# Self-attention's row maxima, turned into rows by one matmul, copied by ScalarE, and added by one-hot weights in the 32-row strips

## The reference

```
q, k, v = heads(x @ Wq), heads(x @ Wk), heads(x @ Wv)     # bias and rotary turn in the first only
scores  = einsum('bhqd,bhkd->bhqk', q, k) / sqrt(16)
probs   = softmax(scores)                                  # exp(scores - max over k), then divided by the sum
x       = x + concat(einsum('bhqk,bhkd->bhqd', probs, v)) @ Wout
```

## Time and profile before

| | us |
|---|---|
| three executions, median (lowest, highest) | 1425.71 (1423.34, 1426.29) |
| the profiled execution, its own time | 1422.83 |
| span of the profile | 1420.9 |
| TensorE clock granted, mean of the span | 0.983 of full |
| PE busy, share of the span | 94% |
| DVE, ACT, POOL busy | 70%, 55%, 26% |

### The profile page before, as it was taken

One profiled execution on the slowest core, in us unless ns is written; L12 is line 12 of the kernel. 1 busy time (PEld: TensorE's weight loads), 2 busy tenths in 40 slices (PEclk: granted clock), 3 DMA queues, 4 the chain that ended last, 5 costly groups with the idle time before them and its releaser, 6 DMA issues. The chain is left out here.

```text
span 1420.9 us, 41741 instructions
## 1 busy us (share of the span) xinstructions
PE 1329.2 (94%) x15796; PEld 1197.8 (84%) x15796; DVE 1001.7 (70%) x2423; ACT 782.4 (55%) x1569; POOL 371.4 (26%) x458
## 2 busy tenths in 40 slices
PE   5999999799979999998999999889999999689887
PEld 5889889699969999998898999768888888578777
DVE  5888888455554545453777777677777777788885
ACT  2655555355545445453555565545555556377786
POOL 1212212011111212110000000055555555134442
PEclk9999999899989999999999999999999999899999
DMA  6000000031000000001000000020000000000000
GB/s 228 3 2 0 0 0 3 7 113 36 30 31 1 1 0 0 0 1 32 22 3 0 0 0 1 2 84 17 16 15 15 15 8 2 1 16 22 30 23 30
DMA packets 16477, 28.72 MB, mean 20 GB/s; under 512 B 3616, under 2 KB 7712, under 8 KB 16000
## 3 DMA queue, kind: packets, MB, share of 16 engines
q1 hardware_dynamic: 16384, 27.44, 5.9%
HBM read 23.24 MB, written 4.19 MB: 19 GB/s over the span
## 5 line engine op out<-in xcount | busy, mean ns | idle before, releaser
L830 DVE TENSOR_REDUCE a_row_max<-a_S 128x4 bf16<-128x512 f32 (+1 forms) x384 | 246.8, 683 | 54.4 <-PE a_S L993 28.8
L723 ACT ACTIVATE a_probs<-a_S 128x512 f32<-128x512 f32 x384 | 208.9, 595 | 112.8 <-PE a_S L1006 60.3
L172 POOL TENSOR_TENSOR all_var_eps<-all_moments,all_ln_eps 128x2 f32<-128x2 f32 x96 | 25.1, 262 | 714.7 <-DVE all_moments L167 714.7
L961 PE MATMUL a_S<-a_qm_hi,all_odd_split 32*128 32x256 f32 x1536 | 187.8, 302 | 7.3 <-DVE a_row_max L830 4.2
L961 PEld LDWEIGHTS a_S<-a_qm_hi,all_odd_split 32*128 32x128 f32 x1536 | 131.5, 183 | 41.5 <-issue 26.2
L687 POOL TENSOR_TENSOR a_shifts<-a_add_mask,a_row_max 128x512 bf16<-128x512 bf16 x128 | 131.0, 1040 | 118.1 <-DVE a_row_max L830 118.1
L952 PE MATMUL a_S<-all_odd_split,a_qm_hi 32*128 32x128 f32 x1536 | 126.8, 283 | 1.7 <-DVE all_odd_weights L938 1.7
L180 DVE TENSOR_SCALAR all_xn<-all_x_res,all_moments,all_rstd 128x256 f32 (+1 forms) x192 | 99.8, 561 | 19.6 <-POOL all_rstd L174 18.8
L961 PE MATMUL a_S<-a_qm_lo,all_odd_split 32*128 32x256 f32 x768 | 108.7, 277 | 0.0
L1019 PE MATMUL a_AV<-a_probs,a_v_pad 128*32 128x128 f32 x3072 | 103.8, 276 | 0.0
L952 PEld LDWEIGHTS a_S<-all_odd_split,a_qm_hi 32*128 32x128 f32 x1536 | 99.8, 185 | 2.6 <-DVE all_odd_weights L938 2.5
(11 more groups left out here) (250 smaller groups left out, 3865.9 us busy)
## 6 DMA issues: line engine op xcount, KB each, us to landing
all_cx<-in_ctx SPq DMA_DIRECT2D x32, 256.0 KB, 2.8
all_x_res<-in_x SPq DMA_DIRECT2D x8, 512.0 KB, 7.7
out_x<-all_x_res SPq DMA_DIRECT2D x16, 256.0 KB, 2.0
b_routed_wi<-in_L_ffn_wi_W SPq DMA_DIRECT2D x1, 1024.0 KB, 5.2
b_routed_wo<-in_L_ffn_wo_W SPq DMA_DIRECT2D x1, 1024.0 KB, 8.0
all_even_weights<-in_L_ffn_W_fc SPq DMA_DIRECT2D x1, 1024.0 KB, 4.9
all_even_weights<-in_L_ffn_W_proj SPq DMA_DIRECT2D x1, 1024.0 KB, 6.9
a_a_raw<-in_L_attn_Wqkv SPq DMA_DIRECT2D x1, 512.0 KB, 4.3
```

The lines of the kernel that those rows point to most:

```text
L723: act.activation(probs[:, t % STEPS, :], S2[t % 2][:], ACT.Exp, scale=DH ** -0.5).then_inc(exp_ok, 1)
L830: dve.tensor_reduce(row_max[:, t % 4, :], S1[t % 2][:].rearrange("p (h k) -> p h k", h=QH), AXX, ALU.max).then_inc(max_ok, 1)
L961: pe.matmul(S2[t % 2][:, c * HV * P:(c + 1) * HV * P], k[par][strip, c, tok], q[par][strip, c, b].rearrange("p h t -> p (h t)"), start=(c ...
```

## The change

Only the self-attention stages change (`not cross` in the code).

- `row_max` becomes a 128 x 128 bf16 tile, zeroed once by POOL; `max_step` writes the four maxima of step t to its columns 32(t mod 4) to 32(t mod 4)+3.
- `turn_max`, new on PE, once a pair of steps: one product with `row_max` as weights and the negated identity moving. It puts the negated maxima into rows (row 32j+h is head h of the step in strip j) in the first 128 columns of bank S1_0. It waits for both maxima of the pair. It stands before `transposes` at t = 0, between `queries` and `av_step` at t = 2, in the middle of `keys` at t = 4, between `values` and `av_step` at t = 6. In the last group it stands right before `av_step` at t = 2 and 6, for lack of the projections.
- `take_max`, new on ACT, once a pair: copies those 128 columns to `maxT` (two buffers, bf16). It stands behind the second exp and behind the copy of `out_high`, if there is one.
- In `scores`, behind the passes of S2, eight products of 32 rows take the place of the eight of `shift_step`: the weights are one column of the constant `strip_rows` (one-hot, 32 rows) broadcast to 128 columns, the moving operand is the strip of `maxT`. They alternate between the two strips and S2 banks of the pair. Both `s2_full` marks now come at their end.
- `scores` waits for `take_max` of the pair before, for S1_0 and for `maxT`, and no longer for anything between S2 and the shift.
- One more constant is loaded at the start (a DMA on SP) and converted by DVE.

```diff
     def __init__(self, nm, a):
-        self.from_dram = {k: a[k] for k in ("ident", "head_mask", "turn_sign")}
+        self.from_dram = {k: a[k] for k in ("ident", "head_mask", "turn_sign", "strip_rows")}
...
         dve.tensor_copy(tiles["ident_b"][:], tiles["ident"][:])
+        dve.tensor_copy(tiles["strip_rows_b"][:], tiles["strip_rows"][:])
...
-    row_max = sb("row_max", [P, 4, QH], FP32 if cross else BF16)
+    row_max = sb("row_max", [P, 4, QH] if cross else [P, P], FP32 if cross else BF16)
+    maxT = None if cross else [sb(f"maxT{i}", [P, P], BF16) for i in range(2)]
...
+            if not cross:
+                pool.memset(row_max[:], 0.0).then_inc(zeroed, 1)
...
+            def take_max(G, t):
+
+                N = G * (STEPS // 2) + t // 2
+                act.wait_ge(maxt_full, N + 1)
+                at_least(act, s2_full, G * STEPS + t - 2)
+                act.activation(maxT[t // 2 % 2][:], S1[0][:, 0:P], ACT.Copy).then_inc(maxt_ok, 1)
...
+                    if not cross and t % 2 == 1 and has_step(G, t):
+                        take_max(G, t - 1)
...
-                dve.tensor_reduce(row_max[:, t % 4, :], S1[t % 2][:].rearrange("p (h k) -> p h k", h=QH),
+                dst = row_max[:, t % 4, :] if cross else row_max[:, 32 * (t % 4):32 * (t % 4) + QH]
+                dve.tensor_reduce(dst, S1[t % 2][:].rearrange("p (h k) -> p h k", h=QH),
...
+            def turn_max(G, t):
+
+                pe.wait_ge(max_ok, G * STEPS + t + 2)
+                pe.matmul(S1[0][:, 0:P], row_max[:], neg_ident_b[:], start=True, stop=True).then_inc(maxt_full, 1)
+
             def scores(G, t, parity):
...
                     at_least(pe, max_ok, T)
+                    if not cross:
+                        at_least(pe, maxt_ok, T_2(G, t))
...
                     at_least(pe, exp_ok, T - 2)
+                    if not cross:
+                        pe.wait_ge(maxt_ok, T_2(G, t))
...
+                if second and not cross:
+                    for at in range(QH):
+                        for u in range(2):
+                            b, j, _ = place(t - 2 + u, parity)
+                            strip = slice(32 * j, 32 * j + 32)
+                            last = pe.matmul(S2[u][:, at * P:(at + 1) * P], strip_rows[strip, at:at + 1].to_broadcast([32, P]),
+                                             maxT[(t // 2 - 1) % 2][strip, :], start=False, stop=(at == QH - 1),
+                                             skip_group_check=True)
+                            if at == QH - 1:
+                                last.then_inc(s2_full, 1)
...
-                    else:
-                        last = pe.matmul(part, row_max[:, t % 4, h:h + 1].to_broadcast([P, P]), neg_ident_b[:],
-                                         start=False, stop=h == QH - 1, skip_group_check=True)
...
                 for m in range(KC):
+                    if m == 1 and between is not None:
+                        between()
...
-                project(FB, WK, kvT_hi, kvT_lo).then_inc(k_full, 1)
+                turn_now = (lambda: turn_max(G, 4)) if not cross and has_step(G, 4) else None
+                project(FB, WK, kvT_hi, kvT_lo, turn_now).then_inc(k_full, 1)
...
-                    if has_step(G, t - 2):
+                    if cross and has_step(G, t - 2):
                         shift_step(G, t - 2)
                         shift_step(G, t - 1)
...
+                    if not cross and t == 0 and has_step(G, t):
+                        turn_max(G, t)
                     if t == 0:
                         transposes(G)
...
+                    if not cross and has_step(G, t) and (t in (2, 6) or t == 4 and not has_window(G)):
+                        turn_max(G, t)
                     if t in (2, 6) and has_step(G, t - 6):
```

More of the change, by code:

```diff
@@ L115, in __init__ @@
             "ones": nm.sb("ones", [P, P]), "minus_half": nm.sb("minus_half", [P, PAIR]), "ln_eps": nm.sb("ln_eps", [P, PAIR]),
+            "strip_rows": nm.sb("strip_rows", [P, QH]), "strip_rows_b": nm.sb("strip_rows_b", [P, QH], BF16),
             "ident_b": nm.sb("ident_b", [P, P], BF16), "neg_ident_b": nm.sb("neg_ident_b", [P, P], BF16),
@@ L551, in attention_stage @@
     v_pad = [sb(f"v_pad{i}", [P, PAIR, H, 2 * DH]) for i in range(2)]
-    row_max = sb("row_max", [P, 4, QH], FP32 if cross else BF16)
+    row_max = sb("row_max", [P, 4, QH] if cross else [P, P], FP32 if cross else BF16)
+    maxT = None if cross else [sb(f"maxT{i}", [P, P], BF16) for i in range(2)]
+    strip_rows = consts["strip_rows_b"]
     av_raw = sb("av_raw", [P, NQ * P])
@@ L582, in attention_stage @@
     vo_full, vo_added = sem("vo_full"), sem("vo_added")
+    maxt_full, maxt_ok = sem("maxt_full"), sem("maxt_ok")
     xn_ok, biased = norm.xn_ok, sem("biased")
@@ L829, in max_step @@
                 at_least(dve, s2_full, T - 3)
-                dve.tensor_reduce(row_max[:, t % 4, :], S1[t % 2][:].rearrange("p (h k) -> p h k", h=QH),
+                if not cross and isinstance(G, int) and G == 0 and t == 0:
+                    dve.wait_ge(zeroed, 3)
+                dst = row_max[:, t % 4, :] if cross else row_max[:, 32 * (t % 4):32 * (t % 4) + QH]
+                dve.tensor_reduce(dst, S1[t % 2][:].rearrange("p (h k) -> p h k", h=QH),
                                   AXX, ALU.max).then_inc(max_ok, 1)
@@ L963, in s2_pass, with T_2 @@
                           skip_group_check=True)
+            def T_2(G, t):
+                return G * (STEPS // 2) + t // 2
+            def turn_max(G, t):
+                pe.wait_ge(max_ok, G * STEPS + t + 2)
+                pe.matmul(S1[0][:, 0:P], row_max[:], neg_ident_b[:], start=True, stop=True).then_inc(maxt_full, 1)
             def scores(G, t, parity):
@@ L998, in shift_step @@
                 T = G * STEPS + t
-                pe.wait_ge(shift_ok if cross else max_ok, T + 1)
+                pe.wait_ge(shift_ok, T + 1)
                 for h in range(QH):
-                    part = S2[t % 2][:, h * P:(h + 1) * P]
-                    if cross:
-                        last = pe.matmul(part, shifts[:, t % 4, h, :], ident_b[:], start=False, stop=h == QH - 1,
-                                         skip_group_check=True)
-                    else:
-                        last = pe.matmul(part, row_max[:, t % 4, h:h + 1].to_broadcast([P, P]), neg_ident_b[:],
-                                         start=False, stop=h == QH - 1, skip_group_check=True)
+                    last = pe.matmul(S2[t % 2][:, h * P:(h + 1) * P], shifts[:, t % 4, h, :], ident_b[:], start=False,
+                                     stop=h == QH - 1, skip_group_check=True)
                 last.then_inc(s2_full, 1)
@@ L1034, in turn_back, with project @@
                 last.then_inc(back, 1)
-            def project(bank, cols, hi, lo):
+            def project(bank, cols, hi, lo, between=None):
                 for m in range(KC):
+                    if m == 1 and between is not None:
+                        between()
                     wcol = slice(cols.start + m * P, cols.start + (m + 1) * P)
@@ L1929, in layout @@
         "head_mask": ((p[:, None] // DH) % HV == np.arange(HV)[None, :]).astype(np.float32),
+        "strip_rows": (p[:, None] % 32 == np.arange(QH)[None, :]).astype(np.float32),
         "turn_sign": np.where(p % DH < DH // 2, -1, 1).astype(np.float32)[:, None],
```

## The result

The change makes the kernel slower: 1441.59 us (median of six executions, 1437.43 to 1445.75) against 1424.94 (six, 1423.34 to 1426.29). The ratio is 1.0113, 95% interval 1.0098 to 1.0128. The executions after also lie farther apart, 8.3 us against 3.0. The profiled one took 1438.89 us, its span is 1437.1, 16.2 more than before; the granted clock is 0.973 on average, 0.983 before. The forecast was 1431, range 1421 to 1441.

What follows compares the result with a forecast made beforehand. PE's list of products was taken to bound the steady groups. Steady groups -2.8, first groups +3.8, last groups +4.1 and start +0.5 summed to +5.6 us: profiled 1428.4, median 1431, range 1421 to 1441.

Steps and rivals of the forecast that it cites:

- rival E: PE's sequencer: extra register steps and waits before strips and `av_step` cost 0.3 us more a group; 1440 us, 13%.
- The eight products: Strip products behind S2 in `scores`: pairs at best pace plus a load gap, saving 0.18 us a pair, 0.72 a group.
- Rival D: The 32-row products do not run in pairs or are paced by their loads: about +21 us, 1447 us, 12%.
- `turn_max`: The new product on PE, three times a steady group, with an uncovered load in `keys`: costs 0.29 us a group.
- (1): `queries` at t = 2 waits for the unshortened transpose chain over ACT and DVE: 0.18 us lost, both stages.
- (2): `scores` at t = 6 waits for `take_max`: 0.10 us lost a group in the first stage, 0.05 in the second.
- (3): `av_step` at t = 6 waits behind `turn_max` for the maxima: 0.15 us lost in the first stage, nothing in the second.
- Rivals B: Faster: the three waits in the steady groups do not arise; -12.0 us there, 1422 us in all, 20%.
- C: No difference: half of the waits, or stage ends half as dear; about 1426.5 us, 20%.
- The first groups: At each stage's start, transposes and scores wait for maxima and the way over ACT: 1.9 us a stage, 3.8 both.
- The last groups: Without projections, `av_step` and scores wait for maxima and ACT: 1.9 us first stage, 2.2 second, 4.1 both.
- The start: A fourth constant's DMA and its cast delay DVE's first work at kernel start: +0.5 us.

Runs made afterwards that it cites:

- experiment 8: Kernel with the old way in the last groups, plus overwritten products filling PE's idle places in group 0 of both stages: 1426.12 us, 0.9999 of before.
- experiment 3: Changed kernel with overwritten products in all idle places of both stages' last groups: 1436.30 us, 1.0072 of before.
- first_behind, experiment 9: Changed kernel with `turn_max` of t = 0 behind the transposes in group 0 of both stages: 1442.14 us, 1.0126 of before.
- the first stage of 2: Changed kernel with overwritten products ahead of `turn_max` at t = 2 and 6 of the last groups: 1437.97 us, 1.0089; first stage's last groups 23.44 us for 26.13.
- Experiment 1: Changed kernel with `turn_max` behind `av_step` at t = 2 and 6 in both stages' last groups: 1436.92 us, 1.0087 of before.
- experiment 4: Kernel before, with only a wait for the group's own maxima added ahead of `av_step` at t = 2 and 6 of the last groups: 1426.51 us, 1.0011.
- ends_old: Changed kernel with the old way in the first and last groups of both stages, the new way in the 14 between: 1423.81 us, 0.9989 of before.
- strips_apart, experiment 10: Changed kernel with the eight strip products ordered four for bank 0, then four for bank 1, not alternating: 1443.03 us, 1.0122 of before.

## Why the prediction was wrong

The sign, the places and the waits were right, and where the waits at the stage ends can be measured at full clock, they came out within 0.1 us; what failed is that the sum had no term for PE's clock. It priced every piece from rows at full clock. The measured time, 1441.59, is close to rival E's 1440, but by luck: E put 0.3 us more a group on PE's sequencer, and 0.08 was found there. Means below are over 12 steady groups, of distances between starts of lines.

- *The eight products*: saved 0.18 a pair, by the forecast. Measured: scores and strips 0.816 + 0.331 us for 0.904 + 0.458, `turn` 0.412 for 0.364, thus 0.17, the 0.05 for `turn`'s load behind the gap among it. Rival D is out: the strips run in pairs, 0.33 with the gap.
- *`turn_max`* and the give-backs: at t = 0 0.065 us (`output` with `turn_max` 1.58 for 1.52). (1) 0.17, as foreseen: transposes to `queries` 2.033 for 2.038; though part of it now shows as a wait for ACT at `scores` of t = 2, where I had called the cover sufficient. At t = 2 0.07. (2) `keys` with `turn_max` 1.71 for 1.56, 0.155 in all, where the sum has 0.11 for the product and 0.10 for the wait. (3) 0.28 at t = 6, where 0.06 and 0.15 had been put. Together +0.07 a group; foreseen 0. In the second stage a group falls from 15.36 to 15.27, by 0.09 and not by 0.20: there t = 6 costs 0.15, where 0.06 had been put. This is not DVE, whose maxima end 0.9 us ahead of `av_step` there, as I had it.
- *The turns of the loop*, which the sum did not have: at four of them a stage, `scores` comes 1.25 to 1.32 us behind `av_step` for 1.04 to 1.09 before. That is 0.96 and 0.90 us a stage, 0.08 a group, and it is part of the 0.28 and of the 0.15 above. Without it t = 6 costs 0.20 and 0.07, close to the 0.21 and 0.06 put there, and these 1.9 us are most of the 2.1 by which the steady groups (-0.7) miss the -2.8. So the register steps of rival E exist, at some 0.1 us each, but they lie bare only where the loop turns. Rivals B and E are out by this, C by the measured time.
- *The first groups*: 1.9 a stage foreseen, 1.5 + 0.3 = 1.8 measured in the second stage at full clock (experiment 8). In the first stage the start with the filling is only 0.15 us longer than before, but the kernel before has 3.4 us at half clock there itself.
- *The last groups*: 1.9 and 2.2 foreseen, 1.8 and 2.2 measured at full clock (experiment 3).
- *The start*: +0.5 foreseen. DVE's first moments start at 5.77 us for 5.55, but the first scores at 23.93 for 23.98: hidden.

**The step that failed** is "There a longer way from maximum to next scores is paid in full": I took it to be paid once, by its own length, and left out what it does to the clock. The waits stand in front of products that then run at half clock. In the profile this is 2.8 + 4.2 us in the last groups (experiment 3; first_behind, with nothing filled but at full clock in the first stage's last groups, has 23.26 us there for the 23.31 of the filled one) and 20.51 - 19.29 = 1.2 in the first of the second stage (experiment 8); the start of the first stage has 21.88 - 19.65 = 2.2 by the same comparison, of which the kernel before has a part of its own. These 10.4 us, with the pieces at full clock (steady -0.7, first 1.8 + 0.15, last 1.8 + 2.2, 5.2 together) make 15.6 of the 16.2. The sum without a clock term was 5.6. The mean clocks of the spans agree in size: 2 x 0.027 x 1437.1 = 78 us at the low level after and 2 x 0.017 x 1420.9 = 48 before; half of the difference, 15 us, bounds what the clock can have cost. These shares are those of one execution: by the medians the first groups cost 6.8 us and the last 8.1, in this profile 5.4 and 11.0, and the fillings give back 5.3 (experiment 3) and 4.4 (experiment 8). That it is the clock, and the idle time that brings it, is shown by the fillings (3 and 8, and the first stage of 2), where the waits stay and the time goes. The rows shown ahead held a warning that I did not read: the mean clock of the span was 0.983, not 1, so low stretches existed, and they lay at starts and ends of stages, where my waits were to go.

The Trainium skill, page "TensorE: Matmul & The Clock Gate", part "HAM oscillation — how this bites in real kernels", tells of a kernel whose PE waits for a DMA between bursts of products, and says that each such wait puts PE back to its slower clock, so that the next burst starts at it. The trace has the same outcome, 0.52 of the full clock from 920.0 us on, behind the waits at 916 to 920 us, but by shorter waits than in that kernel: the longest here is 2.22 us.

What stays open: which idle time lowers the clock. Experiment 1, with 10.00 - 8.31 = 1.7 us idle ahead of 918, lost it, while experiment 4, with 3.3 us, and the kernel before, with 3.56, kept it. Open too is the +1.5 us between the stages, where a low stretch near 425 us lasts 13.6 us for 10.3 before; ends_old has 13.6 there too (418.8 to 432.4) and lost nothing (403.92), so it wanders by itself. And experiment 9.

## What to carry to other kernels

A wait moved to a place where nothing else is queued costs its length once, and perhaps as much again in products that run at half clock behind it: where PE's idle stretches gather, at the fill and drain of a stage, put a clock term into the sum. A change that pays in the steady groups should be switched off in the first and last ones where it costs more there; here that turns +1.1% into -0.1%, with an interval that ends at no change. A wait added inside a loop can also cost its register steps where the loop turns, though it costs nothing elsewhere. Whether a lost microsecond is a wait or a clock is told by filling the wait with products that are overwritten.

## What the runs showed of the hardware

PE's products in different 32-row strips did not keep the program's order: the second four of strips_apart started 0.008 us behind the first and ran beside them, with a pitch of 0.056 within a strip. The Trainium skill, page "TensorE: Matmul & The Clock Gate", part 3, "The mechanism", has products start and end in program order; the marks in experiment 10 disagree.

A wait on PE's sequencer takes some 0.1 us (steps at 130.458, 130.555 and 130.652 us). In the middle of a turn of the loop the same steps run while PE is still at work (145.385 to 145.824 us, with `av_step` in work from 144.994 on, and the next `scores` 1.01 us behind it). Where the loop turns they lie bare: `scores` comes 1.29 us behind `av_step` for 1.045 before, and 0.19 of these 0.25 us are the two new steps.

Idle PE time is not free even off the steady path: 28 waste products in each stage were worth 4.4 us together. What the clock does there differs from one execution to the next: the changed kernel's six lie 8.3 us apart, for 3.0 before.
